# A decoder layer in one kernel: the recurrence in split products with GpSimd's low parts, masked maxima on VectorE, and reordered joints

## The reference

```
x = x + attn_block(norm(x));  x = x + cross_attention(norm(x), context);  x = x + tree_ffn(norm(x))

attn_block(x):
    a  = causal softmax attention of norm(x) (16 heads of 16), through out_w;   x = x + a
    xs = norm(x) * g1 + b1;  vs = 0
    8 times:  u  = tanh(a @ w_ctx + xs @ w_x + b_inl)
              vs = vs + 0.1 * (u - xs - vs);   xs = xs + 0.1 * vs
    x = x + xs
    x = x + gelu(norm(x) @ ff_w1 + ff_b1) @ ff_w2 + ff_b2        (256 -> 1024 -> 256)
```

## Time and profile before

| | us |
|---|---|
| median of 3 runs | 894.53 (893.73 to 896.83) |
| the profiled execution, its own time | 893.74 |
| its span in the profile | 892.0 |
| TensorE busy | 865.2 (97%) |
| VectorE busy | 575.7 (65%) |
| ScalarE busy | 489.6 (55%) |
| GpSimd busy | 176.2 (20%) |
| granted TensorE clock, mean over the span | 0.998 |

### The profile page before, as it was taken

The page is one execution under the profiler, slowest core; times in us unless marked ns, Lnnn a source line. Parts: engine busy times, 40 slices in busy tenths (PEclk is TensorE's granted clock), DMA queues, the critical chain, the costliest instruction groups (busy, mean ns, idle before and its releaser), DMA issues.

```text
span 892.0 us, 11261 instructions
## 1 busy us (share of the span) xinstructions
PE 865.2 (97%) x3967; PEld 526.4 (59%) x3967; DVE 575.7 (65%) x864; ACT 489.6 (55%) x715; POOL 176.2 (20%) x207
## 2 busy tenths in 40 slices
PE   9999999999999999999999999999899999999998
PEld 4665545545455545544446778774345777777775
DVE  4778757757777426678878774366654566665554
ACT  3536566566566755766657555437657433444332
POOL 8712332323222311000011630000015700000000
PEclk9999999999999999999999999999999999999999
DMA  4314405515524114200000000114656200000000
GB/s 148 67 37 75 85 13 98 96 25 96 108 51 93 31 34 165 96 0 1 0 0 22 1 1 1 35 37 87 137 112 156 67 1 25 1 24 1 1 24 24
DMA packets 21879, 46.28 MB, mean 52 GB/s; under 512 B 7896, under 2 KB 10840, under 8 KB 21440
## 3 DMA queue, kind: packets, MB, share of 16 engines
q1 hardware_dynamic: 19136, 43.17, 21.4%
q10 hardware_dynamic: 2080, 1.27, 0.6%
q0 software_dynamic: 608, 1.12, 0.6%
HBM read 17.04 MB, written 2.29 MB: 22 GB/s over the span
## 4 chain that ended last, share of the span: by engine, by line
PE 84%; DVE 5%; ACT 3%; issue 2%; DMA 2%; POOL 1%; SPq 1%; ACTq 0%; DVEq 0%; POOLq 0%
PE psum L1959 12%; PE psum L1721 9%; PE psum L349 9%; PE psum L350 8%; PE psum L351 8%; PE psum L1760 8%; PE psum L1743 8%; PE psum L1687 3%; PE psum L1662 2%; PE psum L1873 2%; PE psum L1724 2%; PE psum L1647 1%; PE psum L1639 1%; PE psum L1946 1%; PE psum L2162 1%
## 5 line engine op out<-in xcount | busy, mean ns | idle before, releaser
L1171 DVE TENSOR_REDUCE part_max<-psum 128x4 f32<-128x512 f32 x288 | 185.5, 686 | 71.0 <-PE psum L1721 56.4
L867 ACT ACTIVATE prob<-psum 128x1024 f32<-128x1024 f32 (+1 forms) x192 | 145.4, 809 | 85.9 <-PE psum L1743 85.4
L1721 PE MATMUL psum<-k,nat_hi 128*128 128x512 f32 x288 | 119.0, 452 | 2.5 <-ACT nat_lo L814 1.2
L1743 PE MATMUL psum<-q,k 128*128 128x512 f32 (+3 forms) x384 | 96.3, 354 | 0.3 <-ACT prob L867 0.3
L1079 ACT ACTIVATE silu<-psum,wt_bias 128x512 f32<-128x512 f32 x64 | 40.5, 684 | 101.9 <-PE psum L351 93.7
L1721 PEld LDWEIGHTS psum<-k,nat_hi 128*128 128x128 f32 x288 | 50.9, 188 | 62.7 <-issue 50.7
L699 POOL TENSOR_SCALAR_AFFINE_SELECT prob<-prob 128x256 f32<-128x256 f32 x128 | 52.3, 415 | 166.0 <-ACT prob L867 164.8
L1760 PE MATMUL psum<-prob,vq 128*32 128x512 f32 (+3 forms) x768 | 81.8, 498 | 1.3 <-POOL prob L699 1.2
L1743 PEld LDWEIGHTS psum<-q,k 128*128 128x128 f32 x384 | 65.2, 189 | 20.5 <-ACT prob L867 8.6
L1580 DVE TENSOR_TENSOR masked_lo<-masked,masked_hi 128x1024 fp32r<-128x1024 f32 x32 | 41.4, 1295 | 42.1 <-ACT masked_hi L1086 42.1
L349 PE MATMUL psum<-masked_hi,wt_hi 128*128 128x512 f32 x128 | 56.2, 439 | 1.2 <-DVE masked_lo L1580 1.2
(11 more groups left out here) (181 smaller groups left out, 1597.5 us busy)
## 6 DMA issues: line engine op xcount, KB each, us to landing
k<-nat_hi SPq DMA_DIRECT2D x92, 64.0 KB, 2.3
xq<-xq_b SPq DMA_DIRECT2D x36, 128.0 KB
q<-nat_hi SPq DMA_DIRECT2D x32, 128.0 KB, 2.3
wt<-in_wt SPq DMA_DIRECT2D x8, 512.0 KB, 4.0
nrm<-in_xT SPq DMA_DIRECT2D x4, 512.0 KB, 8.8
k<-nat_lo SPq DMA_DIRECT2D x32, 64.0 KB, 2.3
q<-nat_lo SPq DMA_DIRECT2D x16, 128.0 KB, 2.3
nrm<-stage SPq DMA_DIRECT2D x32, 64.0 KB, 2.3
```

What stands on the lines that cost most here:

```text
L867: act.activation(prob[:, s % 2, p, :, q0:CH], psum[:, 2 * p:2 * p + 2, q0:CH], ACT.Exp, scale=SCALE)\
L1171: dve.tensor_reduce(part_max[:].rearrange("q (j p i) k -> q p j i k", j=2, p=2)[:, :, :, i, kt], bank(5 + unit_slot[n, u] % 3).rearrange(" ...
L1721: mm = pe.matmul(heads, rounded(nat_hi[:, m, i * P:(i + 1) * P]), k1[:, qd, :, kt * P:(kt + 1) * P], start=True, stop=i != kt)
L1743: mm = pe.matmul(bank(2 * p + j)[:, q0:CH], k2[:, qd, p, j, kt * P:(kt + 1) * P], q2[:, qd, p, c * CH + q0:(c + 1) * CH], start=True, stop ...
```

## The change

Four things are changed.

1. **Recurrence.** `wx01` is split once by GpSimd into `wx_hi` and `wx_lo`. For n >= 1 TensorE computes a chunk step as 12 fp32r products (hi*hi, hi*lo of the state, lo of the weight*hi; two `k`, two `m`) in place of 4 fp32 ones. The state's high parts `y_hi` are two more copies per chunk step on ScalarE, placed behind the tanh of the next chunk step (`high_chunk(*behind)`); the low parts `y_lo` are two subtractions per chunk step on GpSimd (`state_low`, both operands in SBUF). TensorE waits for `y_low` where it waited for `y_ready`.
2. **Mask.** For all diagonal units but 11 (the 8 of pass 0 and 3 of pass 1), the bf16 mask product is gone, and VectorE does four `tensor_tensor_reduce` of 128x128 (add the mask, take the maximum) in place of one reduction of 128x512.
3. **`x0`** is loaded once TensorE has finished the recurrence (its storage now holds `y_hi` till then), and GpSimd's eight additions follow that.
4. **Joints.** `square`/`deviation` of norm 3, chunk 1, and the high parts of the first hidden tiles move in the first feed-forward chunk; variance, mean and spread move by one or two products; `widen` goes from VectorE to GpSimd, `own_part` and `same_head` (`head_tables`) are made earlier; the tree weights are loaded in cross attention's passes 3, 4 and 6 instead of 5 to 7 and after; 12 instead of 14 opening dummy matmuls.

```diff
@@ block.sync
-            sp.wait_ge(ln2.var, ln2.at + NCH)
+            sp.dma_start(wt_bias[:], a["wtb"]).then_inc(wt_bias_in, 16)
+            sp.wait_ge(z_ps, UNITS * NITER)
             sp.dma_start(x0[:], a["xT"]).then_inc(x0_in, 16)
-            sp.dma_start(wt_bias[:], a["wtb"]).then_inc(wt_bias_in, 16)
...
-                if n == 5:
+                if n == 3:
                     sp.wait_ge(xq2_in[0], q_loaded(3))
                     load_tree(0)
+                if n == 4:
+                    load_tree(1)
                 if n == 6:
-                    load_tree(1)
-                if n == 7:
                     sp.wait_ge(xq2_in[1], q_loaded(7))
                     load_tree(2)
+                    load_tree(3)
@@ block.gpsimd
+            pool.wait_ge(wx01_ready, 1)
+            pool.tensor_copy(rounded(wx_hi[:]), wx01).then_inc(wx_set, 1)
+            pool.wait_ge(wx_set, 1)
+            pool.tensor_tensor(rounded(wx_lo[:]), wx01, wx_hi[:], ALU.subtract).then_inc(wx_set, 1)
             pool.memset(xvq[:], 1.0).then_inc(zeros_set, 1)
+            def state_low(n, u):
+                pool.wait_ge(y_high[u % 2], again_at(n, u // 2 * 2 + 1) // 2)
+                pool.tensor_tensor(rounded(y_lo(u)), state(n + 1)[:, u % 2, unit_at(u)], y_hi[:, u, :], ALU.subtract)\
+                    .then_inc(y_low, 1)
+            for n, c in AGAIN:
+                for u in (2 * c, 2 * c + 1):
+                    state_low(n, u)
+            pool.wait_ge(z_ps, UNITS * NITER)
...
+            widen(0)
             split_weights(0)
+            widen(1)
+            split_weights(1)
             spread_cross(2)
-            split_weights(1)
@@ block.scalar
+            def high_chunk(n, c):
+                for u in (2 * c, 2 * c + 1):
+                    act.wait_ge(y_ready, done_at(n, u))
+                    act.activation(rounded(y_hi[:, u, :]), state(n + 1)[:, u % 2, unit_at(u)], ACT.Copy)\
+                        .then_inc(y_high[u % 2], 1)
...
-            for n, c in SCAN[2:]:
+            for (n, c), behind in zip(SCAN[2:], [None] + SCAN[2:]):
                 drive_chunk(n, c)
+                if behind in AGAIN[:-1]:
+                    high_chunk(*behind)
+                if (n, c) == AGAIN[-1]:
+                    high_chunk(n, c)
                 if n < NITER - 1:
                     set_chunk(n, c)
@@ block.vector
+                if i == kt and not masked_in_psum(n, u):
+                    for p in range(2):
+                        for j in range(2):
+                            at = (2 * p + j) * P
+                            ins = dve.tensor_tensor_reduce(
+                                psum[:, 5 + unit_slot[n, u] % 3, at:at + P],
+                                psum[:, 5 + unit_slot[n, u] % 3, at:at + P], caus_f[:], 1.0, -3e38,
+                                ALU.add, ALU.max, accum_out=part_max[:, 16 * j + 8 * p + i, kt:kt + 1])
+                    ins.then_inc(mx_free, 1)
+                    return
@@ block.tensor
-            run_on(14)
+            run_on(12)
...
-                if i == kt:
+                if masked_in_psum(n, u):
...
-                    pe.wait_ge(y_ready, done_at(n - 1, 2 * c + 1))
-                    pe.wait_ge(z_set, again_at(n - 1, 2 * c + 1))
+                pe.wait_ge(wx_set, 2)
+                pe.wait_ge(y_low, again_at(n - 1, 2 * c + 1))
+                pe.wait_ge(z_set, again_at(n - 1, 2 * c + 1))
                 for m in range(KT):
-                    for k in range(KT):
-                        mm = pe.matmul(bank(2 * c + m), wx01[:, k, m * P:(m + 1) * P], state(n)[:, k, cols_of(c)],
-                                       start=False, stop=k == 1, skip_group_check=True)
+                    for part in range(3):
+                        for k in range(KT):
+                            w = (wx_lo if part == 2 else wx_hi)[:, k, m * P:(m + 1) * P]
+                            y = y_lo(2 * c + k) if part == 1 else y_hi[:, 2 * c + k, :]
+                            mm = pe.matmul(bank(2 * c + m), rounded(w), rounded(y), start=False,
+                                           stop=part == 2 and k == 1, skip_group_check=True)
```

More of the change, by code:

```diff
@@ L75, in with_low, with lent @@
             return sb(name, shape, F32, stack), low
+        def lent(name, shape):
+            with ExitStack() as lent_stack:
+                return sb(name, shape, F32, lent_stack)
         def sem(name):
@@ L197, in layer, with y_lo @@
         wff_hi = sb("wff_hi", [P, KT * FF + FT * D])
+        y_lows[0] = lent("y_lo0", [P, 4, CH])
         tree_hi = sb("tree_hi", [P, 2, KT, CH])
+        def y_lo(u):
+            return y_lows[u // 4][:, u % 4, :]
         xk_raw = stage[:].rearrange("p h n -> p (h n)")[:, 0:KT * 4 * CK]\
@@ L255, in layer @@
         begun = sem("begun")
+        wx_set, y_low = sem("wx_set"), sem("y_low")
+        y_high = [sem(f"y_high{m}") for m in range(KT)]
         xq_ps, xq_hi_s, xq_free, xk_ps, xk_hi_s, xk_free, xv_ps, xv_done = [
@@ L334, in layer, with masked_in_psum @@
                         bank_users.append((qk_raw, qk_at(*_ct) + 1))
+        def masked_in_psum(n, u):
+            return self_units[u][0] == self_units[u][1] and (n == 0 or (n == 1 and u < LEAD))
         def slot_free(at):
@@ L987, in xq_high, with hidden_after @@
                     .then_inc(xq_hi_s, 1)
+            def hidden_after(c, m):
+                return (() if m < 3 else (0, 1, 2) if m == 3 else (m - 1,)) if c == 0 else (m - 1,) if m > 0 else ()
             for c in range(NCH):
@@ L996, in _ @@
                         act.activation(hid[:, m, :], bank(ff1_bank(m)), ACT.Gelu, bias=v_("ffb1", m)).then_inc(gelu, 1)
-                    if m > 0:
-                        act.wait_ge(gelu, FT * c + m + 4)
-                        act.activation(rounded(hid_hi[:, m - 1, :]), hid[:, m - 1, :], ACT.Copy).then_inc(hid_h, 1)
+                    if c == 0 and m == 1:
+                        square(ln3)(1)
+                    if c == 0 and m == 2:
+                        deviation(ln3)(1)
+                    for i in hidden_after(c, m):
+                        act.wait_ge(gelu, FT * c + i + 5)
+                        act.activation(rounded(hid_hi[:, i, :]), hid[:, i, :], ACT.Copy).then_inc(hid_h, 1)
                     if m == 6 and c == 0:
@@ L1416, in _ @@
                         third_low((1, 3)[c])
+                    if m == 5 and c == 2:
+                        head_tables()
                     if m == (5, 5, 4, 4)[c]:
@@ L1507, in _ @@
                     xq_low(2, 0)
-                if g == 9:
-                    invert_cross(1)
-                    widen(1)
                 if g == 10:
@@ L1534, in _ @@
                     xq_low(3, g - 4)
-                if g in (6, 14):
-                    invert_cross({6: 0, 14: 2}[g])
-                if g == 5:
-                    dve.tensor_reduce(own_part[:], ident[:].rearrange("p (h s) -> p s h", s=HD), AX_X, ALU.add)\
-                        .then_inc(part_set, 1)
-                    join_heads()
-                if g == 6:
-                    widen(0)
-                if g in (7, 8, 10):
-                    normalize_part({7: 0, 8: 1, 10: 3}[g])
+                if g in (6, 9, 14):
+                    invert_cross({6: 0, 9: 1, 14: 2}[g])
+                if g in (8, 9, 10):
+                    normalize_part({8: 0, 9: 1, 10: 3}[g])
                 if g == 11:
@@ L1721, in unit @@
                 mm = pe.matmul(heads, rounded(nat_hi[:, m, i * P:(i + 1) * P]), k1[:, qd, :, kt * P:(kt + 1) * P],
-                               start=True, stop=i != kt)
-                if i == kt:
+                               start=True, stop=not masked_in_psum(n, u))
+                if masked_in_psum(n, u):
                     mm = pe.matmul(heads, ident_b[:],
@@ L2038, in _ @@
                         xq_projection(1, 0)
-                    if c == 0 and m == 2:
+                    if c == 0 and m == 4:
                         variance(ln3)(1)
-                    if c == 0 and m == 4:
+                    if c == 0 and m == 6:
                         spread_out(ln3)(1)
-                    if m == (4, 4, 1, 1)[c]:
+                    if m == (5, 4, 1, 1)[c]:
                         if c == 0:
@@ L2068, in _ @@
                         beside_last(k)
-                    if c == 0 and k in (5, 7):
-                        (variance, spread_out)[(k - 5) // 2](ln3)(3)
+                    if c == 0 and k in (6, 7):
+                        (variance, spread_out)[k - 6](ln3)(3)
                 mm.then_inc(ff2_ps, 1)
```

71 lines of the change are left out of this document (42 added, 29 removed).

## The result

| kernel | median us | range | ratio to before (95% interval) |
|---|---|---|---|
| before | 895.14 | 893.73 to 896.83 | |
| changed | 930.34 | 929.61 to 932.26 | 1.0394 [1.0372, 1.0415] |

Slower by 3.9%; forecast were 920 us and a range of 903 to 940. The profiled execution of the changed kernel has a span of 928.7 us, that of the kernel before 892.0.

What follows compares the result with a forecast made beforehand. TensorE, busy 97% of the span, was taken as the bound. Recurrence +35, mask -5, x0 and joints -4 make +26 on the profiled 893.74 us, 919.7; with the median 0.8 above, 920 us, range 903 to 940.

Steps and rivals of the forecast that it cites:

- Recurrence, +35: Recurrence: GpSimd's subtractions and VectorE's instructions act as one resource, 4.6 us a chunk step; 32.5 us slower plus 2.5 idle.
- ledger of 137.8 us: Recurrence, first to last low part: 56 subtractions at 1.1 us plus 126 VectorE instructions at 0.605 us.
- bound of +43: Recurrence: upper bound of the loss, at 1.24 us per subtraction, each handed over with no overlap.
- TensorE's clock: Recurrence, rival: the clock falls partly to 1.2 GHz; +12 for half of the steps, +23 for all, 932 to 943 us; 12%.
- Mask, -5: Self attention: 12.2 us of TensorE products go, VectorE takes 1.44 us per diagonal unit; 5 us saved in all.
- lower bound of 1.16: Self attention: least VectorE time per diagonal unit, starts 0.20 us apart plus 0.09 for a readout; would give -12 us.
- estimate of 1.80 us per unit: Self attention: VectorE's time per diagonal unit by the skill's formula, taken as upper bound; a sum 10 us higher.
- `x0` and joints, -4: Behind the recurrence: late x0 additions cost 2 us, idle time cleared at the joints gives -6; bounds -8 to +3.
- the first idle time I had counted on: Feed-forward part: TensorE's 3.4 us idle before `variance`, half of which earlier loads and splits should clear.
- two slow rivals: VectorE bounds self attention, 930 us, 17%; TensorE's clock falls in the recurrence, 932 to 943 us, 12%.
- the bound of self attention: Self attention, rival: VectorE becomes the bound with units at 1.8 us, +5 in place of -5, 930 us; 17%.
- The other side: Recurrence, rival: the engines do not exclude each other, the step is ScalarE's 3.15 us, 878 us in all; 11%.

Runs made afterwards that it cites:

- memset version: The changed kernel with GpSimd's 56 low-part subtractions replaced by memsets of the same low parts, all waits kept: 886.11 us, ratio 0.9883.

## Why the prediction was right

**Recurrence, +35, measured +39.1.** The mechanism and its price held: a step of 4.6 us was forecast and 4.60 is in the trace; VectorE's pairs and `y_lo`'s 1.65 us came as written; TensorE's idle time was 1.6 us in most steps (1.8 forecast), 2.7 in some and next to nothing where the half clock had stretched its work. The ledger of 137.8 us from first to last low part measured 142.8 (361.6 to 504.4 us). VectorE is idle for 5.1 us of it, 4.5 of them in one wait for the first tanh of chunk 2 (376.85 us), where I had allowed 2.5; the work itself is the 137.8 us of the sum. Most of the rest, 1.8 us, is the last products at the half clock, which I had left to a rival. The bound of +43 was worked out with 1.24 us for half of 2.53, which is 1.27 and gives +44. The memset version shows the cause: the same waits without the read give 886 us.

**TensorE's clock.** The rival was right that it falls and wrong in size: 20.5 us at the half clock, not half of the steps. In most of them TensorE waited anyway. The chain passes TensorE at the half clock twice: in the products from 492.65 to 499.03 us, behind which VectorE idles only 0.58 us, and in the last ones, which are what reached the end.

**Mask, -5, measured -4.9, in part by luck.** The unit took 0.96 us, below my lower bound of 1.16: the readout, for which I had added 0.09, costs nothing beside the next quarter. At such a price I had promised -12. I had compared VectorE's busy time of a pass with TensorE's; VectorE was busy 26.6 of 29.98 us and still cost 1 us a pass. Longer waits of TensorE for the maxima are 3.8 of the 6.9 us; where the rest goes is not shown. Two errors cancelled. The Trainium skill, VectorE: DVE Perf Modes (The TRN2 errata), has (N + 151) / 0.96 ns for an fp32 `tensor_tensor` add, confirmed there at 512 and 2048 columns; 291 ns for 128 is an estimate by it. The trace has 320 ns for the add-and-maximum, but starts 0.25 us apart, so the estimate of 1.80 us per unit, which adds up lengths, does not stand.

**`x0` and joints, -4, the step that failed.** What lies behind the recurrence measured +2.5. Feed-forward came out at -2.0, but most of that is not the joints': the mask alone, with the old joints, shortens it from 123.9 to 122.2 us, both with one stretch of half clock of 3.4 us, by a wait before the mean of 1.8 instead of 3.4 us (the first idle time I had counted on; why the mask shortens it is open). With the new joints and no split it is 122.3: no half clock, but 1.3 us more of waits. At the trees' first products GpSimd's low weights cost TensorE 1.3 us instead of 2.9, as I had hoped, but 1.9 instead of 1.2 us for `masked_lo` and 1.0 us for `xprob` came in its place, and the stage is as long as before. In cross attention, where I counted a gain for VectorE without `widen`, they lost 4.4 us (5.2 in the pair without the split). I looked at the two idle times that earlier loads and splits would fill. I did not ask what is queued behind the splits on GpSimd, nor which small transfers would be issued right behind the loads.

**Sum.** 26 was forecast, 36.7 measured on the profiled executions: 4 from the recurrence, 6.5 from `x0` and the joints. The 930 us lie outside the 905 to 925 us that I gave my own forecast its 55% for; they are in the range because it took in two slow rivals, and neither came about (VectorE did not become the bound of self attention, and the clock cost about 2 us). That the first of them also reads 930 us is chance. **The other side**, 878 us, comes within 8 us of the version in which the two engines do not meet: 886 with the memset. The joints are some 7 of these 8.

## What to carry to other kernels

Before work moves to GpSimd beside a VectorE that is busy with instructions of two SBUF operands, count the two as one engine: add VectorE's instructions and GpSimd's with any SBUF read, each at its measured price, and compare with the bound of the stage. An engine's split that saves its time only in the steady state is best begun after the fill and ended before the drain, where nothing covers its extra latency. An idle time that an earlier transfer or split would fill must be weighed with everything that stands behind that step on its queue, small transfers included: here it came back elsewhere, twice.

## What the hardware did that I had not expected

- A GpSimd copy with one SBUF operand delays VectorE too: 0.41 us per 512 columns, against 1.1 us for the subtraction with two; a memset delays it by nothing (pairs at 1.29 us).
- The readout of VectorE's accumulator (0.14 us) lies beside the next instruction: quarters of 128 columns start 0.25 us apart.
- From 50 us of the span on, eleven of the kernels here have 17 idle times of TensorE of 3.4 to 4.8 us; 16 of them had a stretch at the half clock that began within them or less than 1 us from them, 3.4 or 6.8 us long (once 10.2). The work in such a stretch loses half of its time, up to 3.4 us (once 4.9). The one without is at 361.2 us in the kernel with the low parts on VectorE; shorter idle times of 1.5 to 2.7 us were sometimes followed by 3.4 us at the half clock too (the kernel before at 529.5 us).
- The small transfer `xq<-neg_max` lands 2.3 to 2.4 us after its issue elsewhere. In the five cases (in three of the kernels) where it was issued 0.6 us behind a load of tree weights it took 4.4 to 7.3 us.
